# Attention with linear features: the first two score quads of the next chunk move to the front of their eighths

## The reference

```python
h = _ln(x, g1, beta1)
q = _phi((h @ wq).reshape(b, s, H, DH), proj)      # H = 16 heads, DH = 64
k = _phi((h @ wk).reshape(b, s, H, DH), proj)      # _phi = elu(. @ proj) + 1
v = (h @ wv).reshape(b, s, H, DH)
...
kv = kv + k_t[..., :, None] * v_t[..., None, :]    # running sums over the tokens
num = jnp.einsum('bhd,bhde->bhe', q_t, kv)
den = jnp.einsum('bhd,bhd->bh', q_t, ksum) + 1e-06
```

## Time and profile before

| | |
|---|---|
| median of three runs | 2528.15 us |
| profiled execution | 2524.87 us |
| its span in the trace | 2523.1 us |
| PE matmul busy in the span | 2212.0 us, 88% |
| DVE, ACT, POOL busy | 1784.6 us (71%), 1529.7 us (61%), 1469.6 us (58%) |
| HBM, mean over the span | 62 GB/s |

### The profile page before, as it was taken

How to read it: one execution, slowest core, us unless ns; L and a number is a source line. 1 busy time by engine, 2 the same in 40 slices (tenths; PEclk the granted TensorE clock), 3 DMA queues, 4 the chain that set the end, 5 groups by cost and what they waited for, 6 DMA issues and landing times. The chain is left out here.

```text
span 2523.1 us, 64867 instructions
## 1 busy us (share of the span) xinstructions
PE 2212.0 (88%) x24112; PEld 1729.1 (69%) x24112; DVE 1784.6 (71%) x3983; ACT 1529.7 (61%) x2890; POOL 1469.6 (58%) x1449
## 2 busy tenths in 40 slices
PE   3799999999999999999989985899999999994764
PEld 2577777788777787778778874466666666662653
DVE  3477777777777777777777775478787888874443
ACT  3576777677766767677666664656565665651332
POOL 1466666666666667667666653045555565556676
PEclk8899999999999999999999998899999999997897
DMA  3344444444444434344344333011212121101775
GB/s 113 102 124 118 116 129 120 114 127 122 114 121 128 110 101 110 101 109 106 96 110 105 82 91 124 17 60 60 68 47 82 43 76 37 41 22 32 160 138 71
DMA packets 323207, 236.42 MB, mean 94 GB/s; under 512 B 40345, under 2 KB 288141, under 8 KB 322896
## 3 DMA queue, kind: packets, MB, share of 16 engines
q1 hardware_dynamic: 286640, 197.30, 28.8%
q0 software_dynamic: 23808, 21.74, 4.9%
q10 hardware_dynamic: 12448, 13.24, 1.7%
HBM read 73.32 MB, written 82.58 MB: 62 GB/s over the span
## 5 line engine op out<-in xcount | busy, mean ns | idle before, releaser
L964 POOL TENSOR_TENSOR lo<-z,hi 128x512 f16<-128x512 f32 x256 | 306.2, 1196 | 283.2 <-DVE hi L873 250.9
L1849 POOL DMA_INDIRECT slot_dram<-xt,slot_u x256 | 267.3, 1044 | 77.4 <-issue 77.4
L542 PE MATMUL pF<-nh,qk_h 128*128 128x256 f16 x1024 | 281.7, 275 | 8.4 <-DVE nl L861 4.4
L543 PE MATMUL pF<-nh,qk_l 128*128 128x256 f16 x1024 | 281.3, 275 | 0.0
L544 PE MATMUL pF<-nl,qk_h 128*128 128x256 f16 x1024 | 281.2, 275 | 0.0
L788 ACT ACTIVATE sh<-sm 128x512 f16<-128x512 f32 x256 | 160.0, 625 | 97.4 <-DVE sm L894 92.9
L976 POOL TENSOR_TENSOR ol<-on,oh 128x256 f16<-128x256 f32 x256 | 172.2, 673 | 60.6 <-ACT oh L811 60.6
L868 DVE SCALAR_TENSOR_TENSOR z<-pF,z 128x512 f32<-128x512 f32 x256 | 175.1, 684 | 21.4 <-ACT z L771 17.4
L983 POOL TENSOR_TENSOR kvl<-kvacc,kvh 128x260 f16<-128x260 f32 x192 | 157.8, 822 | 53.4 <-ACT kvh L819 53.4
L894 DVE TENSOR_TENSOR sm<-pS,mask 128x512 f32<-128x512 f32 x256 | 174.7, 682 | 17.4 <-PE pS L628 16.8
L542 PE MATMUL pO<-vh,sh 128*128 128x65 f16 x1024 | 120.1, 194 | 67.1 <-issue 47.8
(11 more groups left out here) (298 smaller groups left out, 8387.6 us busy)
## 6 DMA issues: line engine op xcount, KB each, us to landing
w_w<-in_x SPq DMA_DIRECT2D x128, 256.0 KB, 2.8
qdh<-hi SPq DMA_DIRECT2D x512, 64.0 KB, 2.1
qdl<-lo SPq DMA_DIRECT2D x512, 64.0 KB, 2.1
ks<-hi SPq DMA_DIRECT2D x256, 64.0 KB, 2.4
ks<-lo SPq DMA_DIRECT2D x256, 64.0 KB, 2.1
slot_dram<-blank ACTq DMA_DIRECT2D x8, 1360.0 KB, 6.6
xg<-slot_dram SPq DMA_DIRECT2D x40, 272.0 KB, 3.2
x_dram<-x SPq DMA_DIRECT2D x32, 256.0 KB, 2.4
```

Source lines behind the costliest of these rows:

```text
L542: pe.matmul(out, wh, mh, start=first, stop=False, skip_group_check=True)
L543: pe.matmul(out, wl, mh, start=False, stop=False, skip_group_check=True)
L964: nc.gpsimd.tensor_tensor(lo[:, n % 2, :, :], z[:, units(w, FEATS, n) % ZS, :, :], hi[:, n % MOVES, :, :], ALU.subtract).then_inc(fl_ready, 1)
L1849: nc.gpsimd.indirect_dma_start(io["slot_dram"], bass.IndirectOffsetOnAxis(slot_u[:, i % XT, c, k:k + 1], 0), xt[:, i % XT, c, :], None, bo ...
```

## The change

In the eighths g = 2 and 3, where quads 0 and 1 of the next chunk are made, `scores` comes before the early dense use, `outputs` and `turn`; and their `scores_split` comes where `scores` stood, in front of `outputs_split`. The eighths g = 0 and 1 keep their order. No instruction is added or removed, and every engine follows the new order.

```diff
@@ -398,6 +398,9 @@
                     if s == 2 and real(ahead):
                         step("x0", ahead)
                         step("normed", ahead)
+
+                    if g >= 2 and quad is not None:
+                        step("scores", *quad)
                     for what in early:
                         use(u, *what)
                     step("outputs", i, c, g)
@@ -410,8 +413,10 @@
                         step("turn", i - 1, CH - 1, g + 2)
                     for what in early:
                         finish(u, *what[:2])
-                    if quad is not None:
+                    if g < 2:
                         step("scores", *quad)
+                    elif quad is not None:
+                        step("scores_split", *quad)
                     step("outputs_split", i, c, g)
```

## The result

The changed kernel takes 2551.32 us (median of 4, 2548.14 to 2555.21), the kernel before 2528.11 us (4 runs, 2526.76 to 2528.81). The ratio is 1.0093, with a 95% interval of 1.0075 to 1.0111: 23 us slower. The profiled execution took 2548.14 us, its span 2546.1 us against 2523.1. The granted clock doesn't explain the difference: it is 0.99 and 1.00 in the attention (110 to 1540 us) and 0.93 behind it in both traces. One execution of a later kernel, that of eighths 6 and 7, took 9519.95 us at a granted clock of 0.225 and is not in its ratio; every other execution is.

A forecast was written before the change was run, and what follows sets the result against it. Bound: a loop of scores in eighth 0, work up to hi of block 4, then SP's copies. 29 waits, each 0.61 us later, give +17.7 us; with the runs' 3.3 us offset, 2546 us, own range 2536 to 2555.

The forecast's parts named there:

- The front: From scores of quad 2 in eighth 0 to hi of block 4: mask before DVE's division delays it 0.60 us.
- hi of block 3: Eighth 2: z up to 0.2 us late, absorbed by hi's 1.22 us; taken as 0, bounds 0 to 0.2.
- The count, 29: PE's scores waiting on the DMA of ks: 29 waits, each taken 0.61 us later, +17.7 us.
- SP's run: From first copy of block 4 to the scores in eighth 0: stays 19.5 us long.
- sl beside POOL: Eighth 3, DVE: sl meets POOL's xl, ends near 589.1 instead of 588.84, still inside the wait for vh.
- PE's gain in eighth 4: Outputs g = 0 find sl earlier, 1.1 to 1.4 us of 1.65; PE leaves the eighth some 1.2 us earlier.
- The new wait in eighth 6: PE, 1.2 us ahead, waits at the front of eighth 6, scores on sm: 1 to 1.8 us.
- The DMA wait: PE's scores of quad 2 in eighth 0, waiting for the copies: grows from 1.1 to 2 to 3 us.
- the sign that I had named, doubled or more: Sign of a right forecast: PE's DMA wait at scores doubled or more.
- Rival A: The loop is PE's, so its waits on "issue" and sl shrink: -40 or -20 us, 2488 to 2508; 20%.
- Rival B: Block 4's z set by the tie with outputs alone, kvacc's delay caught by vh: no change, 2528; 10%.
- Rival C: POOL meets hi of block 4, or hi of block 6 slips: 1.1 us a unit, 2561; 12%.

The follow-up runs named there:

- that of eighths 6 and 7: The kernel before with the move made only in eighths 6 and 7, eighths 2 and 3 left as before: 1.0018 (1.0000 to 1.0036).
- the eighths-2-and-3 kernel: The kernel before with the move made only in eighths 2 and 3, eighths 6 and 7 left as before: 1.0070 (1.0044 to 1.0096).
- the dose: The kernel before with three more small DVE operations (dn) in front of the division: of eighth 3, 1.0066; of eighth 7, 1.0013.
- the two kernels with vh in front of oh: ACT takes vh before oh in eighth 3: in the kernel before, 0.9996; with scores and mask at the front and splits late, 1.0035.

## Why the prediction was right

The sign, the stage and the mechanism were right; the time forecast was 5 us too low.

- The front: forecast 0.61 us a unit, measured 0.55 in each kind (15.0 us over 30 units in place of 17.7). The mask does cost 0.60 us in front of the division. In front of that, z of block 3 is 0.18 us late in the medians, which the forecast allowed for (up to 0.2), and hi of block 3 takes 1.00 us and not 1.23. I had taken the two together at 0 with bounds of 0 to 0.2 us of loss; they gave back 0.06. The count, 29, was low by one or two.
- SP's run: forecast unchanged. Its median is unchanged; the sum of 31 is 3.5 us more, 3.0 of it in the last two. There some pairs of copies took up to 2.4 us to issue in place of 1.25, as one did in the unit of the earlier trace rows too (2.19 us at 608.55). The same sum lies between 596.4 and 607.0 us in the experiments that leave SP alone, so this is most likely spread and no effect of the change.
- sl beside POOL: the Trainium skill (GPSIMD Engine Reference, Specifications) names contention with GpSimd for a DVE instruction with two SBUF inputs, which sl is. The trace agrees: sl took 0.97 us and ended at 594.26, and vl started at 594.35. So it was covered, with 0.09 us to spare, as forecast.
- PE's gain in eighth 4: the "issue" wait is gone, 0.37 us remains at block 4's product, and the wait on sl fell from 16.2 to 4.6.
- The new wait in eighth 6: forecast 1 to 1.8 us in each unit. The size is right (1.7 us), but it comes only in every second unit, 15 waits and 24.6 us. In the units between, the key transposes of eighth 5 wait 0.95 us instead; they are 14.6 of the 33.1 us on ot, which were 18.3.
- The DMA wait: forecast 2 to 3 us a unit, measured 50.9/31 = 1.6. Behind a unit with the wait of eighth 6 it is 2.2 us, as forecast, and behind the others 1.1, as before. So the sign that I had named, doubled or more, did not quite come, though the mechanism did. Why the two kinds of unit differ stays open.
- Rival A (PE's loop) falls with the eighths-2-and-3 kernel and the dose: PE's largest wait was taken away and the time rose. Rival B (the delay is caught) falls with the fronts. Rival C did not come: hi of block 4 lasted 0.43 us in all 30 units of both traces.
- What the sum lacked: the 3.5 us of SP's runs, and 3.5 us behind the attention, most likely the spread between executions too, though the changed kernel lies at its edge: from the last scores to the end it took 978.6 to 981.4 us in the traces of the eight experiments on the other chips, 979.9 before and 983.4 after. These 7.0 us and the 0.9 in the first and last units, less the 2.7 by which the fronts came out under the forecast, make up the 5 us that the time is above it.

## What to carry to other kernels

Of the largest wait of the busiest engine, ask whether anything behind it would start sooner; here a second wait of that engine, repeated once a unit for the same copies, said no before anything was built. Count a moved operation where it lands in its own engine's list, even if PE is the busiest: 0.6 us in a list of DVE that was 78% busy over the unit cost 0.55 us in one eighth and nothing that could be told in another. And where two lines end in a tie, shortening one is worth nothing (look for the third before building both), and each of them alone can make the same loss. So when an experiment gives back the right time, look in its trace whether it came the same way.

## What the runs showed of the hardware

A copy issued by ACT holds up ACT's computing: four copies, 2.87 us without an instruction. DVE's difference with two inputs in SBUF (sl) took 0.69, 0.97, 1.15 and 1.41 us in the same kernel family, the long ones beside a running POOL operation, so moving it sooner need not make it end sooner: in the two kernels with vh in front of oh it began 0.5 and 0.7 us sooner in the second kind of unit and ended 24.13 and 24.10 us after the scores of eighth 0, where it was 24.13 before. And one chip took 2652 us for the kernel that took 2528 to 2533 on the others. The four profiles made there show the extra time behind the attention: from the last scores to the end it took 1102 to 1110 us at a granted clock of 0.89, against 979 to 983 us at 0.93 to 0.94 on the others, while the attention ran at 0.98 to 1.00 on all of them.
